# A decoder layer on one core: gate-bias rows made in the delta stage, feed-forward loads in order of first use, three chunks' statistics taken inside the first feed-forward tiles

## What is computed

```python
x = x + delta_rule_attention(layernorm(x), ...)          # 16 heads, recurrent, chunked
x = x + set_attention(layernorm(x), ctx_2048, ...)        # top 2 of 64 sets for each token
x = x + ffn(layernorm(x), ...)

def set_attention(...):      # scores over 64 sets, the best two of those allowed, softmax of two
    return jnp.einsum('bsn,bnd->bsd', weights, set_states)

def ffn(x, gate_w, gate_b, val_w, val_b, out_w, out_b):
    gate = silu(bit_linear(x, gate_w, gate_b))
    val = bit_linear(x, val_w, val_b)
    return bit_linear(gate * val, out_w, out_b)

def bit_linear(x, w, b):     # x rounded to 8 bit steps of its row's maximum, w to -1, 0, 1 times its mean size
    return einsum('bsd,hd->bsh', x_rounded, w_ternary) + b
```

## Time and profile before

| what | value |
|---|---|
| median of 3 runs | 2422.05 us (2418.88 to 2422.3) |
| the profiled execution's own time | 2418.03 us |
| its span, first to last instruction | 2416.1 us |
| mean granted TensorE clock | 0.983 |
| busy: PE, DVE, ACT, POOL | 2316.4, 2118.5, 1429.4, 1066.2 us |

### The profile page before, as it was taken

How to read it: one execution, slowest core, us unless ns; L and a number is a source line. 1 busy time by engine, 2 the same in 40 slices (tenths; PEclk the granted TensorE clock), 3 DMA queues, 4 the chain that set the end, 5 groups by cost and what they waited for, 6 DMA issues and landing times. The chain is left out here.

```text
span 2416.1 us, 55384 instructions
## 1 busy us (share of the span) xinstructions
PE 2316.4 (96%) x19873; PEld 1638.6 (68%) x19896; DVE 2118.5 (88%) x4579; ACT 1429.4 (59%) x3891; POOL 1066.2 (44%) x1543
## 2 busy tenths in 40 slices
PE   5899999999999999999999999999999999888998
PEld 3676767777776767676767677777767777673554
DVE  8999999998989999898989898989898989658786
ACT  5566666656565656666666666665555555433665
POOL 3634354444534344544344444434354535214564
PEclk9999999999999999999999999999999999888999
DMA  5211122222212112222122222221111111003000
GB/s 139 64 40 45 43 54 52 55 52 55 53 50 46 48 45 63 61 56 56 44 58 60 64 62 63 61 57 40 32 35 37 22 37 22 17 11 126 23 23 27
DMA packets 289390, 120.76 MB, mean 50 GB/s; under 512 B 211510, under 2 KB 267094, under 8 KB 288604
## 3 DMA queue, kind: packets, MB, share of 16 engines
q1 hardware_dynamic: 289116, 117.21, 18.7%
HBM read 85.42 MB, written 31.74 MB: 48 GB/s over the span
## 5 line engine op out<-in xcount | busy, mean ns | idle before, releaser
L1448 DVE SCALAR_TENSOR_TENSOR d_y<-bank,d_cw,d_y 128x508 f32<-128x508 f32 (+2 forms) x576 | 422.3, 733 | 6.7 <-ACT d_y L1203 1.2
L776 POOL TENSOR_TENSOR d_V<-d_tok,d_kinv 128x640 f32<-128x640 f32 (+1 forms) x128 | 130.8, 1042 | 333.6 <-issue 331.2
L792 POOL TENSOR_SCALAR d_ms<-d_sso 128x4 f32<-128x4 f32 x64 | 14.5, 227 | 565.3 <-ACT d_junk L1341 565.3
L1626 DVE SCALAR_TENSOR_TENSOR x<-bank,x 128x512 f32<-128x512 f32 x256 | 173.5, 678 | 48.4 <-PE bank L1016 48.4
L1203 ACT ACTIVATE d_y<-bank,d_cw 128x512 f32<-128x512 f32 x192 | 131.2, 684 | 88.9 <-PE bank L857 86.1
L1326 ACT ACTIVATE d_thg<-bank 128x384 f32<-128x384 f32 x128 | 62.3, 487 | 202.4 <-PE bank L971 200.1
L1612 DVE SCALAR_TENSOR_TENSOR d_on<-d_O,d_rn,d_gate 128x192 f32<-128x192 f32 x256 | 160.3, 684 | 0.0
L822 POOL TENSOR_SCALAR d_K<-d_tok,d_Em 128x96 f32<-128x96 f32 x256 | 148.6, 597 | 0.1
L1252 ACT ACTIVATE d_tok<-bank 128x384 f32<-128x384 f32 x256 | 125.7, 491 | 34.3 <-PE bank L873 30.3
L1210 ACT ACTIVATE d_th<-d_y 128x512 f32<-128x512 f32 x192 | 121.6, 633 | 36.4 <-DVE d_y L1454 28.0
L741 POOL TENSOR_TENSOR d_Gm<-cst,gh 128x512 f16<-128x512 f32 x128 | 140.0, 1113 | 0.1
(11 more groups left out here) (341 smaller groups left out, 7118.0 us busy)
## 6 DMA issues: line engine op xcount, KB each, us to landing
lt_blocks<-d_LT SPq DMA_DIRECT2D x64, 256.0 KB, 2.7
d_fw<-turned_gate_w SPq DMA_DIRECT2D x32, 256.0 KB, 3.2
d_XT<-x_blocks SPq DMA_DIRECT2D x128, 64.0 KB, 2.4
d_X<-x_blocks SPq DMA_DIRECT2D x128, 64.0 KB, 2.4
d_fw<-turned_val_w SPq DMA_DIRECT2D x32, 256.0 KB, 3.0
d_fw<-turned_out_w SPq DMA_DIRECT2D x32, 256.0 KB, 2.9
d_st<-in_L_attn_Wg_dram SPq DMA_DIRECT2D x16, 384.0 KB, 4.1
ternary<-d_ft SPq DMA_DIRECT2D x48, 128.0 KB, 2.2
```

Source lines behind the costliest of these rows:

```text
L776: last = nc.gpsimd.tensor_tensor(V[q][:, :, lo:hi], tok[q][:, :, at:at + hi - lo], over(kinv[:, :], 2, hi - lo), ALU.mult)
L1448: nc.vector.scalar_tensor_tensor(out=yy[:, :, tap:], in0=pp[:, :, 0:P - tap], scalar=cw[:, ds(st.kp, 1), t, 3 - tap], in1=yy[:, :, tap:], ...
L1626: nc.vector.scalar_tensor_tensor(out=xs, in0=bank[(4, 7, 6, 5)[i]][:, :], scalar=1.0 / (SO * SW), in1=xs, op0=ALU.mult, op1=ALU.add).then_ ...
```

## The change

It touches five things. (1) The load of the gate bias, the six operations and the DMA of `gate_rows` go to the delta stage: the load behind the one of `b_q`, the operations to the head of step NS - 2 on VectorE, the DMA and a wait for it to the end of SyncE's list. (2) SyncE's loads of the third stage are issued in another order, and `woT` and the output bias `ob` count on a semaphore of their own, `out_in`, for which TensorE waits ahead of the first `output` and GpSimd ahead of its first tile. (3) `finish` is split into `add(c)` and `moments(c, tiles)`; chunk 0 does both at once, of chunks 1, 2 and 3 only `add` stays in the set part. (4) `moments` of chunks 1 to 3 is done inside turns u = 0 to 5, two tiles in each, between largest(u, 0) and norm(u+2), and `spread(1)` to `spread(3)` follow the products of tiles 1, 3 and 5 on GpSimd. (5) `outputs(3)` writes banks 4, 5, 6 and 3, so that its first three products don't wait for `added` of chunk 2; the waits for `added` move along.

```diff
+OUT_AT = ((0, 1, 2, 3), (4, 5, 6, 3))
...
+            sp.dma_start(gb[:, :], io["L0_ffn_gate_b"].rearrange("(p j) -> p j", p=P)).then_inc(s["set_in"], 16)
...
+            sp.wait_ge(part_done, 6)
+            sp.dma_start(rows_out.rearrange("r (p j) -> p r j", p=P), gpart[:, :, :]).then_inc(s["block_in"], 16)
+            sp.wait_ge(s["block_in"], 64)
...
+                if n == NS - 2:
+                    nc.vector.reciprocal(gr[:, :], gam[:, 0:1]).then_inc(part_done, 1)
...
-            sp.dma_start(gb[:, :], io["L0_ffn_gate_b"].rearrange("(p j) -> p j", p=P)).then_inc(s["ctx_in"], 16)
-            for name, at in (("val", "vb"), ("out", "ob")):
-                sp.dma_start(keep[at][:, :], io[f"L0_ffn_{name}_b"].partition_broadcast(P)).then_inc(keep["ffn_in"], 16)
             sp.wait_ge(keep["tern_out"], 16 * N_J)
...
+            sp.dma_start(keep["wgT"][:, :, :].rearrange("p k (f d) -> p (k f) d", d=D), keep["tern"][0]).then_inc(keep["ffn_in"], 16)
             sp.wait_ge(s["made"], 2)
             for lo, n in ((0, 3), (3, 2), (5, 1)):
-                sp.dma_start(keep["grow"][lo:lo + n, :], rows[0:n, :]).then_inc(keep["ffn_in"], 16)
+                sp.dma_start(keep["grow"][lo:lo + n, :], keep["rows"][0:n, :]).then_inc(keep["ffn_in"], 16)
+            sp.dma_start(vb[:, :], io["L0_ffn_val_b"].partition_broadcast(P)).then_inc(keep["ffn_in"], 16)
+            sp.dma_start(keep["wvT"][:, :, :].rearrange("p k (f d) -> p (k f) d", d=D), keep["tern"][1]).then_inc(keep["ffn_in"], 16)
+            sp.dma_start(woT[:, :, :], keep["tern"][2]).then_inc(keep["out_in"], 16)
+            sp.dma_start(ob[:, :], io["L0_ffn_out_b"].partition_broadcast(P)).then_inc(keep["out_in"], 16)
...
+                if t < 6 and t % 2:
+                    spread(t // 2 + 1)
                 residual(t)
...
-                    if c:
+                    if 0 < c < 3:
                         pe.wait_ge(s["added"], B * (c - 1) + i + 1)
-                    nc.tensor.matmul(bank[i][:, :], wT[c % 2][:, i, :], ctxs[:, i, :], start=True, stop=True).then_inc(s["o_done"], 1)
+                    if c == 3 and i == 3:
+                        pe.wait_ge(s["added"], B * 2 + 4)
+                    nc.tensor.matmul(bank[OUT_AT[c // 3][i]][:, :], wT[c % 2][:, i, :], ctxs[:, i, :], start=True, stop=True).then_inc(s["o_done"], 1)
...
-            finish(2)
+            select(2)
+            add(0)
+            moments(0, range(B))
+            share(2)
+            select(3)
+            add(1)
+            share(3)
             norm(0)
-            finish(3, lambda: quantize(0))
+            add(2)
+            quantize(0)
             norm(1)
-            v.wait_ge(keep["ffn_in"], 128)
+            add(3)
+            v.wait_ge(keep["ffn_in"], 96)
...
                 if now:
                     largest(u, 0)
+                if u < 6:
+                    moments(u // 2 + 1, (0, 1) if u % 2 == 0 else (2, 3))
                 if u + 2 < NT:
                     norm(u + 2)
```

More of the change, by code:

```diff
@@ L532, in stage_delta_rule @@
     wt, w0, set_var, set_rstd, ss_ = (keep[k] for k in ("wt", "w0", "set_var", "set_rstd", "set_s"))
+    gb, gr, gs, gres, gpart, rows_out, part_done = (keep[k] for k in ("gb", "gr", "gs", "gres", "gpart", "rows", "part_done"))
     st, wa, wo, nw, cw, mone, phalf, mhalf, XTb, Y16, Y32, YJ, X, XT, idh, GTh, nround, img, s = (keep["delta"][k] for k in (
@@ L1888, in _ @@
             split(0)
-            spread(3)
-            pool.wait_ge(keep["ffn_in"], 128)
+            pool.wait_ge(keep["out_in"], 32)
             for t in range(NT):
@@ L1954, in hidden @@
                 if t == 0 and f < 2:
-                    pe.wait_ge(s["added"], B * (CH - 1) + f + 1)
+                    pe.wait_ge(s["added"], B * 2 + f + 1)
                 for k in range(KC):
@@ L1960, in hidden @@
                 if t == 0 and f < 2:
-                    pe.wait_ge(s["added"], B * (CH - 1) + f + 3)
+                    pe.wait_ge(s["added"], B * 2 + 3 if f == 0 else B * 3 + 4)
                 for k in range(KC):
@@ L1968, in turn_a @@
                 past(pe, ffn["aqT_ready"], 2 * t - 1 + h)
+                if t == 0:
+                    pe.wait_ge(s["added"], NT)
                 for k in range(8):
@@ L1974, in output @@
                 past(pe, ffn["out_ready"], t)
+                if t == 0:
+                    pe.wait_ge(keep["out_in"], 32)
                 for k in range(NH):
@@ L1981, in _ @@
             turn_h(0)
-            pe.wait_ge(keep["ffn_in"], 128)
+            pe.wait_ge(keep["ffn_in"], 96)
             for u in range(NT + 2):
@@ L2090, in share, with add, moments @@
                 set_share(nc, v, s, c, eg[:, c - 2, :], den[:, c - 2, :], w0)
-            def finish(c, between=None):
+            def add(c):
                 v.wait_ge(s["w0_ready"], 2 * c + 2)
-                def add(i):
+                for i in range(B):
                     v.wait_ge(s["o_done"], B * c + i + 1)
                     t = i * CH + c
-                    nc.vector.scalar_tensor_tensor(out=x_sb[:, t, :], in0=bank[i][:, :], scalar=w0[:, c, i:i + 1], in1=x_sb[:, t, :],
+                    nc.vector.scalar_tensor_tensor(out=x_sb[:, t, :], in0=bank[OUT_AT[c // 3][i]][:, :], scalar=w0[:, c, i:i + 1], in1=x_sb[:, t, :],
                                                    op0=ALU.mult, op1=ALU.add).then_inc(s["added"], 1)
-                def stat(i):
+            def moments(c, tiles):
+                for i in tiles:
                     v.wait_ge(s["added"], B * c + i + 1)
@@ L2105, in stat @@
                     nc.vector.bn_stats(stats[:, i, :], x_sb[:, i * CH + c, :]).then_inc(s["stat"], 1)
-                add(0)
-                add(1)
-                stat(0)
-                add(2)
-                stat(1)
-                add(3)
-                stat(2)
-                if between:
-                    between()
-                stat(3)
-                for i in range(B):
+                for i in tiles:
                     v.wait_ge(s["stat"], B * c + i + 1)
                     nc.vector.bn_aggr(ffn_mv[:, i * CH + c, :], stats[:, i, :]).then_inc(s["aggr"], 1)
-            select(2)
-            nc.vector.reciprocal(gr[:, :], gam[:, 0:1]).then_inc(s["part_done"], 1)
-            v.wait_ge(s["ctx_in"], 32)
-            v.wait_ge(s["part_done"], 1)
-            nc.vector.tensor_scalar(gs[:, :], gb[:, :], gr[:, 0:1], None, ALU.mult).then_inc(s["part_done"], 1)
-            v.wait_ge(s["part_done"], 2)
-            nc.vector.tensor_copy(gpart[:, 0, :], gs[:, :]).then_inc(s["part_done"], 1)
-            v.wait_ge(s["part_done"], 3)
-            nc.vector.tensor_tensor(gres[:, :], gs[:, :], gpart[:, 0, :], ALU.subtract).then_inc(s["part_done"], 1)
-            v.wait_ge(s["part_done"], 4)
-            nc.vector.tensor_copy(gpart[:, 1, :], gres[:, :]).then_inc(s["part_done"], 1)
-            v.wait_ge(s["part_done"], 5)
-            nc.vector.tensor_tensor(gpart[:, 2, :], gres[:, :], gpart[:, 1, :], ALU.subtract).then_inc(s["part_done"], 1)
-            finish(0)
-            share(2)
-            select(3)
-            finish(1)
-            share(3)
             def norm(t):
@@ L2253, in build @@
                         for name, e in (("pe", nc.tensor), ("act", nc.scalar), ("pool", nc.gpsimd), ("sp", nc.sync))}
+        for name, shape, dt in (("gb", [P, FF // P], F32), ("gr", [P, 1], F32), ("gs", [P, FF // P], F32), ("gres", [P, FF // P], F32),
+                                ("gpart", [P, 3, FF // P], BF16)):
+            keep[name] = ctx.enter_context(nc.sbuf_tensor("gate_" + name, shape, dt))
+        keep["rows"] = nc.dram_tensor("gate_rows", (3, FF), BF16).ap()
+        keep["part_done"] = ctx.enter_context(nc.semaphore("part_done"))
+        keep["out_in"] = ctx.enter_context(nc.semaphore("out_in"))
         keep["set_s"] = {name: ctx.enter_context(nc.semaphore("set_" + name)) for name in SET_SIGNALS}
```

33 lines of the change are left out of this document (15 added, 18 removed).

## The result

| what | before | after |
|---|---|---|
| median, 9 runs each | 2421.19 us | 2427.51 us |
| range of the runs | 2411.13 to 2424.08 | 2423.32 to 2430.64 |
| ratio after / before | | 1.0032, 95% interval 1.0018 to 1.0046 |
| profiled execution, own time and span | 2418.03, 2416.1 | 2428.87, 2427.1 |

A forecast was written before the change was run, and what follows sets the result against it. TensorE was taken to set the steady pace, VectorE the set part's end. Set part -1.7 plus turns +5.0 gave +3.3 us, 2425.3 on the median 2422.05, rounded to 2425; range 2416 to 2429.

The forecast's parts named there:

- the loss in the turns: Feed-forward turns 1 to 6: statistics on the path to the next clip cost 5.0 us, ends 4.4 and 6.5.
- the gain in the set part: End of the set part: turn_h(0) starts at 2202.7 instead of 2204.43, gain 1.7 us, ends 0.8 and 2.6.
- rival A: Set part: the clock falls before outputs(2), whose instructions take 7.64 us; net +5.3, 2427.4 on the median; chance 0.20.
- the clock's fall moved: Set part: a sign that the forecast is wrong; it had the clock falling at 2190.1 again.
- The ring of turns 1 to 6: Path from value(u, 3) to the next clip: 1.35 us of statistics less slack, paid anew each turn.
- Rival C: Feed-forward turns: the statistics fit into VectorE's 2.53 us of spare time; net -1.7, 2420.3; chance 0.15.
- turns 3 to 6: Feed-forward part: each turn pays 1.35 - 0.55 = 0.80 us, 3.20 together.
- The "0" for GpSimd: Turns: spreads of about 1.3 us each fit GpSimd's 5.2 us over, results needed a turn later; cost 0.
- The 0.55 by which outputs(2) was to come late: Set part: select(3), then outputs(2), starts 0.55 us late, since statistics no longer fill the waits between adds.
- the first tile: Start of the feed-forward part: the clock rises as long after the first gate product as before, keeping the whole 1.7.
- Bias rows, loads, DMAs: Delta stage and loads: cost 0 for each; at most 1.3 us for the rows if their cover were gone.
- The waits of (5): Set part: the removed waits for `added` were not what held outputs(3), which starts behind the copy.

The follow-up runs named there:

- e2: Changed kernel with the statistics of turns 0 to 5 moved ahead of value(u, 3); 2424.01 us, ratio 1.0004 to the kernel before.
- e4: Changed kernel with GpSimd's residual of each tile moved to the head of the next tile's work, behind the split; 2433.09 us in one run.
- e12: Changed kernel with statistics ahead of value(u, 3), dummy products in set part and delta stage, and loads in the old order; 2403.30 us, ratio 0.9914 to before.
- e5: Kernel before with only the bias rows' load, operations and DMA moved to the delta stage; 2426.23 us against 2423.73, ratio 1.0012.
- e1: Changed kernel with the statistics of chunks 1 to 3 back in the set part, behind their adds; 2424.77 us against 2423.16 for before, ratio 1.0004.

## Why the prediction was right, and where not

The time lay inside the range and on the side of the forecast, but the loss is 6.3 us where +3.3 had been worked out, and "slower by over 0.2%" had been given only 0.23. Two of its terms lie outside the ends that it gave them: the loss in the turns, 7.1 for 5.0 with an upper end of 6.5, and the gain in the set part, 0.46 for 1.7 with a lower end of 0.8 (against before profiled again it is 1.46, inside the ends). Both errors go the same way, and the total stayed inside the range because its upper end had been set for rival A. By its own signs it was wrong on one count too, since the clock's fall moved. Point by point:

- **The ring of turns 1 to 6.** The mechanism was right: no slack in turn 1, 0.90 and 0.55 in turns 2 and 3, the stall paid anew because value(u, 3) hangs on TensorE. Turn 1 lost 1.38 (1.35 foretold). Turn 2 lost 0.42 (0.45 foretold), and that agreement is luck: its norm had taken 0.85 before, under GpSimd's residual, and now takes 0.55, while the clip takes 0.21 more. Rival C, that 2.53 us of spare time would take them in, was wrong for this place of the statistics; e2 shows that it is right for another.
- **Mis-sized: turns 3 to 6,** 5.3 for 3.2. Of that 0.3 is the pair at 1.42 instead of 1.35. The rest is the step that took norm's and clip's durations unchanged from before, while the later norm ran into GpSimd's residual: 0.68 more in turns 3 and 5, 0.21 in 4 and 6 (e4). The "0" for GpSimd had looked at its spare time only.
- **Mis-sized: the set part,** 0.46 for 1.7. The 1.7 was counted from `turn_h(0)`, which was 0.48 earlier after the stage's start (33.26 for 33.74). The 0.55 by which outputs(2) was to come late was 0.40 (17.30 after the stage's start for 16.90). But it had been assumed that the clock falls at 2190.1 again, 19.4 after the stage's start. It fell ahead of outputs(2), so the eight instructions ran wholly at the lower level. That is rival A's mechanism, and it happened; A had left no gain at all, but the eight instructions took 7.16 and not its 7.64. It is no effect of the change, though: before, profiled again, has it too (7.16), with a set part of 36.34, and against that the gain is 1.46.
- **Left out: the first tile.** From the first gate product to value(0, 3), at 2220.45, it took 10.81 instead of 10.48, since the clock came back 5.2 us behind the gate product (2214.9, from the window of 2213.64) and not 4.6. The prediction had let it come back as long after as before; with e4's 2.7 and 9.57 this term differs by more than 1 us between executions.
- **Bias rows, loads, DMAs:** priced at 0. The loads are shown to be free (e12). The rows cost nothing that the runs can tell, with some 2.5 us open (e5).
- **The waits of (5).** "Were not what held outputs(3)" holds. What parts (3) to (5) do together had been seen only in part: the text said that the set part's end hangs on VectorE, and then priced the relief by TensorE's list at the low clock alone.

The sum of the measured terms is -0.46 + 0.33 + 1.38 + 0.42 + 5.3 = +7.0 against the first profile of before. Against the second, whose clock fell as early as after's, the first two are -1.46 and +0.68, and the sum is +6.3. The medians say 6.3.

## What to carry to other kernels

Work that is moved into spare time must be put where the idle time lies, not just into the same turn: the same six pairs of statistics cost 7 us behind value(u, 3) and nothing ahead of it. And it should be asked whether the work was in the way at all: put back in the set part (e1), the statistics cost that part nothing. When a bound moves from one engine to another, look at what the new one suffers from; here it was TensorE's clock, and a few products that nobody reads were worth 7.7 us in the set part, but only after VectorE had been taken off the path. And one profile's end of a long stage is no evidence: profile the old kernel twice before a difference there is explained.
